# First retention layer: the compute engines' loop over sequences replaced by code written out for all sixteen

## The chip, the cores and the metric

The kernel runs on one core of a Trainium2 chip, as one program. The metric is the device time of one execution, in microseconds, lower is better. A core has five engines that run programs of their own and meet only at semaphores: TensorE (PE in the profile; its weight loads are PEld), VectorE (DVE), ScalarE (ACT), GpSimd (POOL) and SyncE (SP), which here only issues transfers. An engine's sequencer reads the engine's program, works out register values, waits on semaphores and hands instructions on.

## What is computed

Two layers, each a retention followed by a mixture of experts, on 16 sequences of 512 tokens with 128 features. The change touches the first retention alone:

```python
q, k = _apply_rotary((x @ Wq.T).reshape(B, T, 4, 32), (x @ Wk.T).reshape(B, T, 4, 32))
v = (x @ Wv.T).reshape(B, T, 4, 64)
q = q * 32 ** (-0.5)
scores = einsum('bhtd,bhsd->bhts', q, k) * decay_mask        # causal, one decay per head
o = einsum('bhts,bhsd->bhtd', scores, v)
o_n = o * rsqrt(mean(o * o, -1) + EPS) * g_norm_w
g = (x @ Wg.T).reshape(B, T, 4, 64)
x = layernorm(x + (o_n * silu(g)).reshape(B, T, 256) @ Wo.T)
# then: two of eight experts are chosen for each token of x
```

The kernel's first stage computes this, chooses the experts of every token and scatters the token rows to DRAM by expert. The experts of layer 0, the second retention, the experts of layer 1 and a last sum with its normalization follow as stages of their own.

## The kernel before

`retention0` gives each engine a program of steps. A step works on up to six sequences at once, each at another point of its way: `z` is sequence s (its transposed input is split in a high and a low part), `a` is s-1 (projections of q, k, v and the gate), `b` is s-2 (scores, states, outputs), `c` is s-3 (gating and transposes), `d` is s-4 (output projection, normalization, router), `e` is s-5 (ranks and rows of the chosen experts). POOL has a seventh, `f`, for s-6. So steps 0 to 20 carry the sixteen sequences through. Below, **score step n** is the stretch of TensorE's program from the scores of sequence n (L879, the first work of step n+2) to those of sequence n+1.

The engines are tied by semaphores that count up. What matters around the start of a score step: TensorE ends the step before with the transposes of `gated_transposes` (L917) and `outputs(b, 3)` (L898 and L901), then computes the scores (L879) into four banks, the ranks (L379 to L387) and the output projection (L937). ScalarE waits for L917 and copies the result (L734), then for `outputs(b, 3)` and squares it (L737). VectorE waits for that square, gates (L786) and masks the new scores (L762). TensorE needs the masked scores before it goes on to the projections of the next sequence (L863). Later in the step TensorE's transposes L330 need ScalarE's normalization L248.

`run_steps` (L79) writes a program. Steps below `2 * first` stand written out, each with the numbers of its sequences as constants. If `first < last`, one `Fori` (L92) follows whose body is two steps, run `last - first` times, with sequence numbers and semaphore counts taken from registers. The steps from `2 * last` on are written out again. In `retention0` `first, last = 3, SEQS // 2` (L603), that is 3 and 8: steps 0 to 5 written out, five iterations for steps 6 to 15, steps 16 to 20 written out. In score steps: 0 to 3 written out, 4 to 13 in the loop (two in an iteration, the even one first), 14 and 15 written out. POOL uses the same numbers; SyncE loops from step 10. `wait_count` (L60) and `Chain.link` (L77) make a wait with a count: of a constant, or in the loop of a register.

Of the kernel before, what the change touches and what calls it, by code (L numbers as in the profile page):

```python
# [16 lines left out]
SEQS, T, D = 16, 512, 128  # L17
# [31 lines left out]
def turn(i, sub, lag, count, unroll):  # L49

    k = sub - lag
    if isinstance(i, int):
        n = unroll * i + k
        return Turn(n, n // 2, n % 2, n // 4, n % 4) if 0 <= n < count else None
    if unroll == 4:
        return Turn(i * 4 + k, i * 2 + k // 2, k % 2, i + k // 4, k % 4)
    return Turn(i * 2 + k, i + k // 2, k % 2)

def wait_count(eng, sem, n):

    if isinstance(n, int) and n <= 0:
        return
    eng.wait_ge(sem, n)  # L63
# [19 lines left out]
def run_steps(eng, first, last, count, lags, body, between=(), unroll=2):  # L83


    total = count + max(lags)
    for s in range(unroll * first):
        body([turn(s // unroll, s % unroll, lag, count, unroll) for lag in lags])
        if s < len(between):
            between[s]()  # L90
    if first < last:
        with eng.Fori(first, last) as i:  # L92
            for sub in range(unroll):
                body([turn(i, sub, lag, count, unroll) for lag in lags])
    for s in range(unroll * last, total):
        body([turn(s // unroll, s % unroll, lag, count, unroll) for lag in lags])

def build(nc, x, x_T, w_proj, wo, gnorm, rope, router0, gate0, up0, down0,
# [9 lines left out]
    with whole:  # L108
# [422 lines left out]
        def retention0():  # L531
            ph = ExitStack()
            with ph:
# [68 lines left out]
                lags = [0, 1, 2, 3, 4]  # L602
                first, last = 3, SEQS // 2  # L603
# [5 lines left out]
                @block.sync  # L609
                def _(sp):  # L610
                    def load(t):

                        wait_count(sp, x_there, t.n - 1)
                        sp.dma_start(xT[t.odd][:], x_T[bass.ds(t.n, 1)].rearrange("b d t -> d (b t)")
                                     ).then_inc(s_x[t.odd], 16)

                    def body(ts):
                        if ts[0] is None:
                            return
                        load(ts[0])  # L620
                        if isinstance(ts[0].n, int) and ts[0].n == 0:
                            sp.dma_start(w_raw[:], w_proj).then_inc(s_wp, 16)
                            sp.dma_start(c_ident[:], ident).then_inc(s_id, 16)
                            for to, src in small:
                                sp.dma_start(to[:] if to is not w_r else to[:, 0:E], src).then_inc(s_w, 16)
                            for to, src in consts:
                                sp.dma_start(to[:], src).then_inc(s_const, 16)
                            sp.dma_start(tri_f[:], tri).then_inc(s_const, 16)
                        if isinstance(ts[0].n, int) and 1 <= ts[0].n <= 4:
                            q = ts[0].n - 1  # L630
                            sp.dma_start(xres[:, q * 16:(q + 1) * 16, :],
                                         x_seq[:, q * 4:(q + 1) * 4].rearrange("p b c d -> p (b c) d")
                                         ).then_inc(s_xr, 16)
                        if isinstance(ts[0].n, int) and 2 <= ts[0].n < 2 + E:
                            load_expert(sp, 0, ts[0].n - 2, s_wx0)

                    run_steps(sp, (2 + E) // 2, last, SEQS, [0], body)
                    tiles.fill(sp)
# [42 lines left out]
                @block.scalar  # L681
                def _(act):
                    def turned_logits(d):
                        act.wait_ge(lgT_mm, d.n + 1)
                        wait_count(act, router.lg_mm, d.n)
                        nc.scalar.copy(lgT[:], T1[:, 0:P]).then_inc(lgT_there, 1)

                    def body(ts):
                        z, a, b, c, d = ts
                        if b:  # L690
                            act.wait_ge(kt_mm, b.n + 1)
                            nc.scalar.copy(kt[:], T1[:, 0:(CH - 1) * P].rearrange("p (c k) -> p c k", c=CH - 1)
                                           ).then_inc(kt_ev, 1)
                        if z:
                            act.wait_ge(s_x[z.odd], z.half * 16 + 16)

                            wait_count(act, g_mm, z.n - 1)
                            nc.scalar.copy(x_hi[z.odd][:], xT[z.odd][:]).then_inc(x_hi_there, 1)
                        if c and not b:
                            act.wait_ge(ogT_mm, c.n + 1)  # L700
                            nc.scalar.copy(ogT[:], TT).then_inc(ogT_ev, 1)
                        if d:

                            wait_count(act, router.sent[d.odd], SCATTERS * d.half)
                            wait_count(act, x1_kept, d.n - 1)
                            norm.apply(act, r, x1[d.odd][:, :, 0:D], d, x1_there)
                        if a:
                            act.wait_ge(v_mm, a.n + 1)
                            nc.scalar.copy(v[a.odd][:], B01.rearrange("p b (c n) -> p (b c) n", c=2)).then_inc(v_ev, 1)
                        if b:  # L710

                            wait_count(act, ch_ss.sem, 2 * b.n - 1)
                            act.wait_ge(o_mm, 2 * b.n + 1)
                            nc.scalar.activation(osq[:, 0:2, :], O.rearrange("p (c n) -> p c n", c=2),
                                                 ACT.Square).then_inc(sq_there, 1)
                        if d:
                            act.wait_ge(router.tp, d.n + 1)
                            nc.scalar.copy(router.xT[:], T0).then_inc(router.xT_there, 1)
                            if not a:
                                turned_logits(d)  # L720
                            act.wait_ge(x1_there, d.n + 1)
                            nc.scalar.copy(xres[:, bass.ds(d.n * CH, CH), :], x1[d.odd][:, :, 0:D]).then_inc(x1_kept, 1)
                            router.copy_rows(act, d, x1_there)
                        if a:
                            act.wait_ge(g_mm, a.n + 1)

                            wait_count(act, og_there, 2 * (a.n - 1))
                            nc.scalar.activation(sg[a.odd][:], B23.rearrange("p b (c n) -> p (b c) n", c=2),
                                                 ACT.Silu).then_inc(g_ev, 1)
                        if d and a:  # L730
                            turned_logits(d)
                        if c and b:
                            act.wait_ge(ogT_mm, c.n + 1)
                            nc.scalar.copy(ogT[:], TT).then_inc(ogT_ev, 1)  # L734
                        if b:
                            act.wait_ge(o_mm, 2 * b.n + 2)
                            nc.scalar.activation(osq[:, 2:4, :], O.rearrange("p (c n) -> p c n", c=2),  # L737
                                                 ACT.Square).then_inc(sq_there, 1)

                    nc.scalar.preload_act_table_set("silu_and_others")  # L740
                    act.wait_ge(s_wp, 16)
                    nc.scalar.copy(w_hi[:], w_raw[:]).then_inc(w_hi_there, 1)
                    run_steps(act, first, last, SEQS, lags, body)

                @block.vector
                def _(dve):
# [97 lines left out]
                        if d:  # L844
                            router.choose(dve, LG, d)

                    run_steps(dve, first, last, SEQS, lags + [5], body)
                    tiles.table(dve)
                    centered.compute(dve)

# [1 line left out]
                def _(pe):  # L852
# [67 lines left out]

                    def body(ts):
                        _, a, b, c, d, e = ts
                        if b:

# [76 lines left out]
                        if b:  # L1001
                            outputs(b, 3)

                    run_steps(pe, first, last, SEQS, lags + [5], body)


        def experts(layer):
# [947 lines left out]
```

## Time and profile before

| | us |
|---|---|
| median of 3 runs | 1414.75 |
| lowest, highest | 1414.15, 1416.67 |
| the profiled execution | 1418.55 |
| its span in the trace | 1416.4 |

The profiled execution is 3.8 us longer than the median, and 2.15 us of it lie outside its span. The page gives busy times of engines over the span. A row of a window gives the same for a stretch; the timeline gives single instructions, with the idle time of the engine before one in brackets and what ended it: an instruction of another engine, "remote" for a semaphore whose raiser isn't told, or "issue" where the engine waited for nothing that the profile shows. In rows with a q behind the engine's name stands work of its sequencer, which isn't counted as busy.

### The profile page before, as it was taken

What the parts mean: (1) busy time and instruction counts of PE and PEld (TensorE: products, weight loads), DVE (VectorE), ACT (ScalarE), POOL (GpSimd) and SP (SyncE); (2) the same over time, 40 slices, a digit from 0 to 9 for tenths busy, and PEclk for the clock granted to TensorE, in tenths of its full rate; (3) what the DMA queues carried; (4) which work ended last, traced back from release to release, by engine and by line L of the source; (5) the groups of instructions that cost most, each with busy time, mean ns of one, the idle gap of its engine ahead of it and who ended that gap; (6) DMA issues with size and microseconds to landing.
All of it is one profiled execution on the core that took longest, in us unless ns stands there. A gap on an engine that the chain in (4) does not pass through costs nothing. (4 is left out here: it accounts for less than half of the span.)

```text
span 1416.4 us, 33456 instructions
## 1 busy us (share of the span) xinstructions
PE 1151.2 (81%) x10358; PEld 1023.1 (72%) x10359; DVE 911.9 (64%) x2572; ACT 718.5 (51%) x1875; POOL 746.8 (53%) x903
## 2 busy tenths in 40 slices
PE   7999999984188888846899999983499999999930
PEld 5887888864188788844676776662499999999930
DVE  4788788864465555514788888755566666666626
ACT  2344344432265555625566666642366666666627
POOL 0266667656446666651146666667244444444446
PEclk9999999986599998977999999985699999999975
DMA  7211112000232222214222112011221111111138
GB/s 230 58 60 45 43 45 71 26 24 31 84 90 88 80 83 82 84 40 141 76 91 84 58 58 75 28 35 58 57 57 53 54 54 56 52 54 54 42 112 266
DMA packets 75408, 102.00 MB, mean 72 GB/s; under 512 B 15154, under 2 KB 51506, under 8 KB 74866
## 3 DMA queue, kind: packets, MB, share of 16 engines
q1 hardware_dynamic: 49586, 60.96, 14.7%
q0 software_dynamic: 17280, 35.69, 7.7%
q10 hardware_dynamic: 8448, 4.20, 1.0%
q8 instruction: 48, 0.79, 0.2%
q14 instruction: 46, 0.38, 0.1%
HBM read 60.93 MB, written 44.11 MB: 74 GB/s over the span
## 5 line engine op out<-in xcount | busy, mean ns | idle before, releaser
L1091 POOL DMA_INDIRECT expert_out<-e_ysb,e_idx x284 | 309.2, 1089 | 309.1 <-ACT e_ysb L1130 180.5
L1239 PE MATMUL banks<-e_x_hi,e_w_hi 128*128 128x256 f32 x852 | 255.9, 300 | 4.6 <-issue 2.4
L1239 PE MATMUL banks<-e_x_hi,e_w_lo 128*128 128x256 f32 x852 | 244.0, 286 | 2.2 <-issue 2.0
L1239 PE MATMUL banks<-e_x_lo,e_w_hi 128*128 128x256 f32 x852 | 243.7, 286 | 2.5 <-issue 2.5
L1249 PE MATMUL banks<-w_dn,e_h 128*128 x1704 | 220.5, 280 | 19.2 <-issue 9.9
L1210 DVE TENSOR_TENSOR e_h<-banks,e_sgl 128x512 f32<-128x512 f32 x213 | 146.8, 690 | 137.0 <-PE banks L1239 75.7
L1249 PEld LDWEIGHTS banks<-w_dn,e_h 128*128 128x128 f32 x1704 | 207.4, 195 | 22.3 <-issue 22.1
L1117 ACT ACTIVATE e_sgl<-banks 128x512 f32<-128x512 f32 x213 | 128.1, 602 | 122.9 <-PE banks L1239 80.0
L1239 PEld LDWEIGHTS banks<-e_x_hi,e_w_hi 128*128 128x128 f32 x852 | 165.9, 195 | 5.8 <-issue 5.7
L1239 PEld LDWEIGHTS banks<-e_x_hi,e_w_lo 128*128 128x128 f32 x852 | 165.5, 194 | 4.7 <-issue 4.7
L1239 PEld LDWEIGHTS banks<-e_x_lo,e_w_hi 128*128 128x128 f32 x852 | 166.0, 195 | 2.8 <-issue 2.6
L1200 DVE TENSOR_TENSOR e_w_lo<-w_gu,e_w_hi 128x512 fp32r<-128x512 f32 (+1 forms) x142 | 136.4, 960 | 39.8 <-ACT e_w_hi L1108 28.9
L451 POOL DMA_INDIRECT scattered<-b_r_x,b_r_idx x128 | 131.1, 1025 | 36.5 <-issue 36.2
L451 POOL DMA_INDIRECT scattered<-a_r_x,a_r_idx x128 | 128.7, 1005 | 36.3 <-issue 36.3
L1108 ACT CAST e_w_hi<-w_gu 128x512 fp32r (+1 forms) x142 | 119.8, 844 | 8.0 <-issue 6.0
L1226 PE MATMUL banks<-c_ident,e_xg 128*128 128x128 f32 x284 | 57.1, 284 | 59.0 <-DMA e_xg<-scattered 58.6
L1111 ACT CAST e_x_hi<-banks 128x256 fp32r<-128x256 f32 x142 | 53.4, 376 | 97.3 <-PE banks L1226 52.2
L1531 DVE TENSOR_TENSOR b_sT<-banks,c_causal 128x1024 f32<-128x1024 f32 x64 | 75.4, 1220 | 23.2 <-PE banks L1609 22.0
L1226 PEld LDWEIGHTS banks<-c_ident,e_xg 128*128 128x128 f32 x284 | 36.7, 147 | 62.1 <-issue 52.3
L1204 DVE TENSOR_TENSOR e_x_lo<-banks,e_x_hi 128x256 fp32r<-128x256 f32 x142 | 59.6, 420 | 29.7 <-ACT e_x_hi L1111 23.1
L664 POOL TENSOR_TENSOR a_inv_rms<-a_mse,c_half 128x16 f32<-128x16 f32 x16 | 53.5, 3341 | 47.6 <-DVE a_mse L779 46.5
L901 PEld LDWEIGHTS banks<-a_v,a_sT 128*128 128x128 f32 x512 | 69.6, 197 | 4.3
(280 smaller groups left out, 2468.7 us busy)
## 6 DMA issues: line engine op xcount, KB each, us to landing
e_xg<-scattered SPq DMA_DIRECT2D x142, 130.0 KB, 1.9
b_cy<-expert_out SPq DMA_DIRECT2D x32, 256.0 KB
f_y<-expert_out SPq DMA_DIRECT2D x32, 256.0 KB, 3.9
expert_out<-e_ysb,e_idx POOLq DMA_INDIRECT x284
a_xT<-in_x_T SPq DMA_DIRECT2D x16, 256.0 KB
out<-f_x ACTq DMA_DIRECT2D x16, 256.0 KB, 4.1
scattered<-in_spare SPq DMA_DIRECT2D x2, 1040.0 KB
scattered<-in_spare SPq DMA_DIRECT2D x16, 130.0 KB
```

What stands on the lines that cost most here:

```text
L451: nc.gpsimd.indirect_dma_start(out=scattered[0:E * REGION, :], out_offset=bass.IndirectOffsetOnAxis(ap=self.idx[t.odd][:, j:j + 1], axis=0 ...
L901: mm = nc.tensor.matmul(O[:, at + h * DV0:at + (h + 1) * DV0], sT[:, h, c, :], v[b.odd][:, c, h * DV0:(h + 1) * DV0], start=(c == 0 and h ...
L1091: nc.gpsimd.indirect_dma_start(out=expert_out, out_offset=bass.IndirectOffsetOnAxis(ap=idx[d.slot][:, i:i + 1], axis=0), in_=ysb[d.slot][: ...
L1108: nc.scalar.copy(w_hi[b.slot][:], w_gu[:, bass.ds(e, 1), :, 0:F].rearrange("p o g f -> p (o g) f")).then_inc(w_hi_there, 1)
L1117: nc.scalar.activation(sgl[bank_of(j, c)][:], GB[bank_of(j, c)][:].rearrange("p (k n) -> p k n", k=2), ACT.Silu).then_inc(sg_there, 1)
L1200: nc.vector.tensor_tensor(w_lo[b.slot][:], w_gu[:, bass.ds(e, 1), :, 0:F].rearrange("p o g f -> p (o g) f"), w_hi[b.slot][:].bitcast(F32), ...
L1204: nc.vector.tensor_tensor(x_lo[b.slot][:], TP[b.odd][:, 0:ROWS], x_hi[b.slot][:].bitcast(F32), ALU.subtract).then_inc(x_ev, 1)
L1210: nc.vector.tensor_tensor(h[c.slot][:, 2 * j:2 * j + 2, :], UB[bank_of(j, c)][:].rearrange("p (k n) -> p k n", k=2), sgl[bank_of(j, c)][:] ...
L1226: mm = nc.tensor.transpose(TP[b.odd][:, i * P:(i + 1) * P], xg[b.slot][:, i, 0:D], c_ident[:])
L1239: mm = nc.tensor.matmul(banks[bank_of(j, c)][:, i * ROWS:(i + 1) * ROWS], w_[c.slot][:, g, f:f + P], x_[c.slot][:], start=(k == 0), stop=( ...
L1249: mm = nc.tensor.matmul(YB[d.odd][:, i * D:(i + 1) * D], h[d.slot][:, f, i * P:(i + 1) * P], w_dn[:, bass.ds(e, 1), f, :].rearrange("p o d ...
L1531: nc.vector.tensor_tensor(sT[h][:, 2 * g:2 * g + 2, :, :].rearrange("p g n t -> p (g n) t"), pairs[2 + g].rearrange("p g (n t) -> p (g n) ...
```

## The change

The programs of ScalarE, VectorE and TensorE in `retention0` are made with `run_steps(..., last, last, ...)` in place of `run_steps(..., first, last, ...)`, so the branch with `Fori` isn't taken and all 21 steps stand written out. GpSimd's and SyncE's programs, the order of the work within a step, buffers, and the other stages stay as they are.

```diff
@@ retention0, scalar
-                    run_steps(act, first, last, SEQS, lags, body)
+                    run_steps(act, last, last, SEQS, lags, body)
@@ retention0, vector
-                    run_steps(dve, first, last, SEQS, lags + [5], body)
+                    run_steps(dve, last, last, SEQS, lags + [5], body)
@@ retention0, tensor
-                    run_steps(pe, first, last, SEQS, lags + [5], body)
+                    run_steps(pe, last, last, SEQS, lags + [5], body)
```

What stands on TensorE after the ranks in the loop's second step, before the change (the names in brackets are semaphores; L946 and L950 set up a wait for the masked scores, L954 one for the outputs' bank):

```order
L943 MATMUL banks<-c_ident,a_kT 128x128 [waits a_ogT_ev]
L943 MATMUL banks<-c_ident,a_kT 128x128 x2
L946 ISA
L950 REGISTER_ALU [waits a_sT_there]
L863 MATMUL banks<-a_x_hi,a_w_hi 128x512 [waits a_x_there]
```

and in a step of the changed kernel:

```order
L943 MATMUL banks<-c_ident,a_kT 128x128 [waits a_ogT_ev]
L943 MATMUL banks<-c_ident,a_kT 128x128 x2
L863 MATMUL banks<-a_x_hi,a_w_hi 128x512 [waits a_x_there,a_sT_there]
```

The two register instructions are gone and the wait on the masked scores stands on the matrix multiply itself.

On ScalarE, at the entry of the loop and in the first step of its body, before the change:

```order
L737 ACTIVATE a_osq<-banks 128x512 [waits a_o_mm]
L92 UNCONDITIONAL_BRANCH
L92 ISA
L692 COPY a_kt<-banks 128x384 [waits a_kt_mm]
L695 ISA
L698 CAST a_x_hi<-a_xT 128x512 [waits a_g_mm,a_x0]
L63 ISA
L63 REGISTER_ALU [waits sent00]
L246 REGISTER_ALU [waits a_x1_kept]
L248 ACTIVATE a_r_x<-a_r,a_n_bias,a_n_rstd 128x128 [waits a_n_inv]
```

and at the same place of the changed kernel:

```order
L737 ACTIVATE a_osq<-banks 128x512 [waits a_o_mm]
L692 COPY a_kt<-banks 128x384 [waits a_kt_mm]
L698 CAST a_x_hi<-a_xT 128x512 [waits a_g_mm,a_x0]
L248 ACTIVATE a_r_x<-a_r,a_n_bias,a_n_rstd 128x128 [waits a_n_inv,a_x1_kept,sent00]
```

The branch and the register instructions are gone; copies, activations and their waits stand in the order in which they stood.

## Rows read from the trace of the kernel before

**Rows 1.** The page's head and part 1: busy time, share, instructions of each engine.

```profile
span 1416.4 us, 33456 instructions
PE 1151.2 (81%) x10358; PEld 1023.1 (72%) x10359; DVE 911.9 (64%) x2572; ACT 718.5 (51%) x1875; POOL 746.8 (53%) x903
```

**Rows 2.** Windows, one for each of score steps 3 to 14: start:end, length, busy times.

```profile
68.26:85.97 17.71, 17.57 (x179) 15.30 (x179) 15.93 (x54) 8.13 (x15) 8.36 (x9) 1.00 0.15 46
...
85.97:105.13 19.16, 18.09 (x180) 15.62 (x179) 15.40 (x51) 7.37 (x15) 13.56 (x17) 1.00 0.21 65
105.13:124.97 19.84, 18.50 (x179) 15.74 (x179) 15.97 (x53) 8.14 (x15) 13.54 (x17) 1.00 0.20 61
124.97:144.91 19.94, 18.52 (x179) 15.75 (x178) 16.01 (x54) 8.15 (x15) 13.55 (x17) 1.00 0.13 40
144.91:163.98 19.07, 17.93 (x180) 15.48 (x179) 15.90 (x53) 8.14 (x15) 13.55 (x17) 1.00 0.13 42
163.98:183.94 19.96, 18.56 (x180) 15.77 (x179) 16.32 (x56) 8.14 (x15) 13.55 (x17) 1.00 0.12 40
183.94:203.09 19.15, 18.17 (x179) 15.72 (x178) 15.66 (x51) 8.14 (x15) 13.54 (x17) 1.00 0.14 42
203.09:223.02 19.93, 18.51 (x179) 15.75 (x178) 16.40 (x54) 8.13 (x15) 13.63 (x17) 1.00 0.13 40
223.02:242.10 19.08, 17.93 (x179) 15.49 (x178) 16.00 (x54) 8.14 (x15) 13.55 (x17) 1.00 0.27 82
242.10:261.44 19.34, 18.05 (x180) 15.61 (x179) 16.43 (x56) 8.27 (x16) 13.55 (x17) 1.00 0.13 43
261.44:280.48 19.04, 17.94 (x179) 15.57 (x179) 15.93 (x54) 8.10 (x15) 13.55 (x17) 1.00 0.09 28
280.48:299.60 19.12, 18.14 (x179) 15.69 (x178) 15.69 (x54) 8.50 (x15) 13.43 (x16) 1.00 0.10 33
```

The columns behind the length are PE, PEld, DVE, ACT and POOL busy time with instructions, then TensorE's granted clock, the DMA share and GB/s.

**Rows 3.** The loop's own line L92, whole program: sequencer instructions, duration ns min/median/max.

```profile
L92 PEldq COMPARE_BRANCH  x23: 83/215/238, 122.8 to 1319.3; - x23
L92 DVEq COMPARE_BRANCH  x25: 50/56/85, 125.6 to 1406.4; - x25
L92 ACTq COMPARE_BRANCH  x25: 40/45/59, 126.5 to 1406.9; - x25
```

**Rows 4.** Timelines of ACT and of DVE as score steps 7 and 8 begin.

```profile
145.45 1.01 ACT L734 COPY a_ogT<-banks 128x1024 f32<-128x1024 f32 x1 [3.32 <-remote]
165.33 1.01 ACT L734 COPY a_ogT<-banks 128x1024 f32<-128x1024 f32 x1 [4.06 <-remote]
...
147.00 0.69 DVE L786 TENSOR_TENSOR a_og<-banks,a_sg 128x512 f32<-128x512 f32 x1 [1.40 <-ACT a_osq L737]
166.96 0.69 DVE L786 TENSOR_TENSOR a_og<-banks,a_sg 128x512 f32<-128x512 f32 x1 [2.21 <-ACT a_osq L737]
```

**Rows 5.** Waits of PE over the loop, 85.97:280.48: us in total, times, longest.

```profile
PE banks L330 <- ACT a_r_x L248: 7.8, 10, 0.9
PE banks L879 <- issue: 3.5, 10, 0.4
```

**Rows 6.** DMA queues of the first pass through the loop's body, 85.97:124.97: packets, MB, share.

```profile
q8 instruction: 3, 0.05, 0.5%
q14 instruction: 2, 0.02, 0.2%
```

**Rows 7.** DMA queues of the later passes, 120:285.

```profile
q1 hardware_dynamic: 1616, 3.29, 6.8%
q14 instruction: 1, 0.01, 0.0%
```

**Rows 8.** The queue q8 in the windows 104.5:105 and 299.8:300.3.

```profile
q8 instruction: 1, 0.02, 11.7%
...
q8 instruction: 1, 0.02, 12.0%
```

**Rows 9.** PE's timeline: end of the scores in score steps 14 and 15.

```profile
282.66 0.58 PE L937 MATMUL banks<-a_won,a_ogT 128*128 128x128 f32 x3
...
302.30 0.40 PE L879 MATMUL banks<-a_qr,a_kT 32*128 32x128 f32 x3 [0.94 <-issue]
306.66 1.63 PE L937 MATMUL banks<-a_won,a_ogT 128*128 128x128 f32 x6
```

## The prediction

> **What bounds the kernel now.** I read the page first: TensorE is busy 81% of the span, the next engine 64% [rows 1]. Then the windows of the stage that is changed, cut at the starts of the scores [rows 2]. In each score step TensorE is busy 17.9 to 18.6 of 19.04 to 19.96 us, VectorE 15.4 to 16.4, GpSimd 13.6, ScalarE 8, and the granted clock is 1.00 (2.4 GHz), so the step goes by TensorE with what it waits for. The reader is to see a pattern in the lengths. Steps 4 to 13 are the loop. The first steps of iterations two to four, which are 6, 8 and 10, take 19.94, 19.96 and 19.93 us; the second steps 7, 9, 11 and 13 take 19.07, 19.15, 19.08 and 19.04. Two don't fit: step 5, a second one, takes 19.84, and step 12, a first one, only 19.34. Step 4, entered without a jump back, takes 19.16. Step 14, written out on all three engines, takes 19.12.
>
> Where the 0.8 us of a long step lie is in the timelines of its start. In step 7 (from 144.91) ScalarE's L734 begins 0.54 us after the scores, in step 8 (from 163.98) 1.35 us after. VectorE's L786 follows at +2.09 and +2.98, idle 1.40 and 2.21 us before it [rows 4]. That delay reaches the masked scores and TensorE's next projections. ScalarE had long been idle, so it is a result of TensorE that comes late by that much. The waits that the profile names on TensorE are the same kind in every step: L330 for ScalarE, 7.8 us in ten steps, and 3.5 us of "issue" inside the scores [rows 5].
>
> **Part 1, the jump back.** On TensorE one L92 branch lasts 215 ns at the median and 238 at most, on VectorE 56, on ScalarE 45 [rows 3]. The work of the latter two hides that: both wait for TensorE around the step's start, 1.40 us even in a short step [rows 4]. On TensorE's own side the branch comes just ahead of the scores, 32 small products that need instructions fast. Four jumps back at 0.24 us are 0.95 us, the lower bound of the gain if the step lengths have another cause. The upper bound is from the step lengths. The loop lasts from 85.97 to 280.48, 194.51 us for ten steps; ten steps like step 14 would be 191.20. The difference is **3.31 us**: 0.76 in iteration one (39.00 less 38.24), 0.77, 0.87, 0.77, and 0.14 in the last. I take the upper value, since the jump back precedes just steps 6, 8, 10 and 12, three of which are 0.8 us longer than their neighbours with the same instructions, and since step 14, even as they are, is short. What is late next in a step of 19.1 us is the chain through VectorE's statistics, GpSimd's power and L248 to L330, which is there in step 14 too.
>
> **Part 2, register instructions.** Waits that were built from registers become waits on constants: on TensorE two or so of the sequencer's instructions go at five places of a step, on the others likewise. A second step of an iteration has these too, and at 19.04 to 19.15 us it is as long as step 14, which has none. So I cost their removal at nothing. What hides it is the time that a long product takes while the sequencer reads on. If that cover is absent at the scores, it is in the 3.5 us of issue time over ten steps [rows 5], and these are the most that it could bring.
>
> **Part 3, code.** The loop's body is fetched once: three packets of queue q8, TensorE's, and two of q14 in the 39.00 us of its first pass [rows 6]. In 120:285, over four more passes, q8 has no packet at all and q14 one [rows 7]. Written out, the eight further steps fetch about four times as much: 12 packets on q8 and 8 or so on q14. As transfers these are nothing, each a few hundredths of a MB. But does TensorE halt when it goes on to a new piece? The steps 0 to 3 and 14 have such fetches and no gap that I can tie to them. Against that, two fetches fall right at the start of scores: one in 104.5:105, ahead of step 5 (105.13), the odd step that is long; and one in 299.8:300.3, in step 15 [rows 8], where TensorE gets its instructions so slowly that L937 begins 7.06 us after the scores' start and not 2.18 as in step 14 [rows 9]. Price of one hit: nothing at the low end, 0.77 us (step 5 less step 7), 4.88 at the high end (7.06 less 2.18). I take nothing, for step 15 has another cause at hand (GpSimd's scatters, unpaced there). The Trainium skill, page "Runtime: NRT & Kernel Launch", section "Instruction fetch mechanics", holds that a sequencer fetches the next block while it runs the present one and that crossing is mostly hidden, which would speak for nothing too. The same section says that a taken branch breaks the prefetch if its target isn't among the pages held and that kernels for this reason rather unroll. By that each of the four jumps back would have its own fetch, and the trace disagrees for TensorE: q8 has none in 120:285 [rows 7].
>
> **Part 4, what isn't changed.** GpSimd and SyncE keep their loops. GpSimd is paced by the others' semaphores and busy 13.6 us of a step [rows 2], so it follows a shorter one. The stage ends in a chain that starts from the last scores, and the following stages start when all engines are through, so 3.3 us saved ahead of step 14 reach the end.
>
> **Sum.** Against the profiled execution: 1418.55 - 3.31 = 1415.24. The same saving from the median of the runs, 1414.75, gives 1411.44; I forecast **1411.5 us**. A measurement here tells about 0.2%, 2.8 us, from no change; the forecast is barely beyond it.
>
> **The rivals.**
>
> *Fetches eat part of the gain.* Of 12 new fetches, if they fall evenly and those within 2 us of the start of the scores count (4 of 19.1 us), 2.5 hit, at 0.77 us 1.9 us; step 5's own 0.77 stays. 3.31 - 0.77 - 1.9 = 0.6 us: **1414.1**. For it: step 5, which no jump explains. Against it: steps 0 to 3.
>
> *The pattern isn't the jump's.* Even and odd sequences use different buffers, and the even ones could be slower by something else in the middle of the stage, or the delay appears only with the profiler on. For it: step 12 follows a jump too and is 0.27 us longer, not 0.8. Against it: step 14 is even and short. Then nothing changes: **1414.7**.
>
> *The change makes it slower.* TensorE's code is no longer all held once the loop has gone round, and a piece that begins in the middle of the scores while GpSimd scatters costs what step 15 lost, 4.88 us [rows 9]. Two such hits in ten steps are 9.8, less 3.3: 1414.75 + 6.5 = **1421**. It decides from one such hit on, since 4.88 is more than 3.31. For it: the fetch lies within 0.7 us of the stall's begin. Against it: step 5, hit likewise, lost 0.77 at most, and GpSimd's unpaced scatters are in step 15 alone.
>
> *More is gained.* Step 3, written out, with the same 179 products, takes 17.71 us [rows 2]. If the loop made all of the difference to 19.1, ten steps would give 14 us more: **1397**. Against it: step 14 is written out and takes 19.12; step 3 differs in GpSimd's load (8.36 us, not 13.6).
>
> **How the numbers follow.** Chances: the forecast 0.43, fetches eating part 0.25, no effect 0.15, slower 0.11, more gained 0.06. The forecast's own range is 1409.5 to 1412.5: below, the issue time of part 2 half saved; above, a third of the gain lost. The range of 8 in 10 also takes in the second and the third case with a run's spread of 1 to 2 us above them, since the runs went from 1414.15 to 1416.67: 1409.2 to 1416.2. Faster by over 0.2% (below 1411.9): 0.37 of the forecast's 0.43, and more gained, 0.43. Within: 0.06, 0.24 and 0.14, so 0.44. Slower: 0.11 and 0.02 of the others, 0.13.
>
> **What would show it.** Right: score steps 5 to 13 all at 19.0 to 19.2 us, L734 about 0.6 us behind the scores' start in even and odd steps alike, some 20 fetches of q8 in the stage, and step 15 as long as before. Rival one: long steps remain, and a fetch of q8 stands within 2 us of each one's start. Rival two: 19.9 us at even steps still. Slower: gaps of issue inside L879 of over 0.9 us, several in a row, in steps before 15. Wrong in another way would be a change after the stage's end, near 388 us: later stages run the same code, but the fetches of TensorE fall at other places in them.

## The result, and the profile after

| | before | changed |
|---|---|---|
| median of 20 runs each, us | 1419.97 | 1414.51 |
| lowest, highest | 1414.15, 1426.18 | 1409.76, 1419.31 |
| profiled execution, us | 1418.55 | 1415.69 |
| its span | 1416.4 | 1413.9 |

The ratio of the changed kernel to the kernel before is 0.9951, 95% interval 0.9935 to 0.9967: faster by 0.49%, or by 4.7 to 9.2 us from end to end of the interval. The medians differ by 5.5. The median of before has moved as well: over 20 runs it is 1419.97, where the first three gave 1414.75.

The page of the changed kernel has the same compute work as [rows 1] and more pieces of code:

```profile
span 1413.9 us, 33103 instructions
PE 1150.6 (81%) x10358; PEld 1022.6 (72%) x10359; DVE 910.2 (64%) x2572; ACT 716.5 (51%) x1875; POOL 742.6 (53%) x903
...
q8 instruction: 59, 0.97, 0.3%
q14 instruction: 51, 0.42, 0.1%
```

Some 350 instructions are gone, none of them on an engine's data path: the counts behind the busy times are those of [rows 1]. The score steps, which answer to [rows 2] (windows by score step 3 to 14; columns as there):

```profile
66.29:84.01 17.72, 17.57 (x180) 15.31 (x179) 15.94 (x54) 8.28 (x15) 8.36 (x9) 1.00 0.16 46
84.01:103.03 19.02, 18.06 (x179) 15.59 (x179) 15.61 (x52) 7.22 (x14) 13.53 (x17) 1.00 0.21 65
103.03:122.15 19.12, 17.98 (x179) 15.53 (x179) 16.32 (x56) 8.14 (x15) 13.53 (x17) 1.00 0.21 63
122.15:141.30 19.15, 18.01 (x180) 15.57 (x179) 15.94 (x54) 8.29 (x16) 13.55 (x17) 1.00 0.14 43
141.30:160.32 19.02, 17.99 (x180) 15.54 (x179) 15.60 (x52) 8.17 (x16) 13.55 (x17) 1.00 0.14 44
160.32:179.38 19.06, 17.97 (x180) 15.59 (x179) 16.29 (x56) 8.28 (x16) 13.51 (x17) 1.00 0.13 43
...
274.52:293.52 19.00, 18.00 (x179) 15.63 (x178) 15.42 (x53) 7.67 (x15) 13.41 (x16) 1.00 0.10 33
```

No step is long now: score steps 4 to 13 take from 84.01 to 274.52, 190.51 us where they took 194.51, and step 14 takes 19.00 where it took 19.12. Step 3, the same code in both kernels, is 17.71 and 17.72.

The starts of steps 7 and 8, on ScalarE and VectorE, which answer to [rows 4]:

```profile
141.14 1.01 ACT L734 COPY a_ogT<-banks 128x1024 f32<-128x1024 f32 x1 [2.56 <-PE banks L917]
142.71 0.60 ACT L737 ACTIVATE a_osq<-banks 128x512 f32<-128x512 f32 x1 [0.55 <-PE banks L901]
...
160.22 1.01 ACT L734 COPY a_ogT<-banks 128x1024 f32<-128x1024 f32 x1 [2.63 <-PE banks L917]
161.77 0.60 ACT L737 ACTIVATE a_osq<-banks 128x512 f32<-128x512 f32 x1 [0.54 <-PE banks L901]
...
143.33 0.69 DVE L786 TENSOR_TENSOR a_og<-banks,a_sg 128x512 f32<-128x512 f32 x1 [1.92 <-ACT a_osq L737]
162.40 0.69 DVE L786 TENSOR_TENSOR a_og<-banks,a_sg 128x512 f32<-128x512 f32 x1 [1.54 <-ACT a_osq L737]
```

L734 begins 0.16 and 0.10 us ahead of the scores (141.30, 160.32), where it began 0.54 and 1.35 behind. L786 is at +2.03 and +2.08, where it was at +2.09 and +2.98. So at L786 a short step has gained 0.06 us and a long one 0.9.

The 2.5 us between the two spans don't all belong to the change. Up to score step 4 the changed kernel's trace is 1.96 us shorter, where both kernels run the same code; score steps 4 to 14 are 4.12 us shorter; and from score step 15 on, 1116.8 us became 1120.4, 3.6 us longer.

### The profile page after: what moved, and what is told of

It reads as the page before. It is cut to its first block and busy times, and to the rows that moved or that the text cites. A ratio compares the mean times of both kernels' runs of the same rounds, so it can differ in the third digit from the quotient of the medians.

```text
span 1413.9 us, 33103 instructions
## 1 busy us (share of the span) xinstructions
PE 1150.6 (81%) x10358; PEld 1022.6 (72%) x10359; DVE 910.2 (64%) x2572; ACT 716.5 (51%) x1875; POOL 742.6 (53%) x903
## 5 line engine op out<-in xcount | busy, mean ns | idle before, releaser
L1204 DVE TENSOR_TENSOR e_x_lo<-banks,e_x_hi 128x256 fp32r<-128x256 f32 x142 | 59.5, 419 | 23.5 <-ACT e_x_hi L1111 17.4
L901 PEld LDWEIGHTS banks<-a_v,a_sT 128*128 128x128 f32 x512 | 69.4, 197 | 4.0
```

Of the source, the lines that this page charges most:

```text
L901: mm = nc.tensor.matmul(O[:, at + h * DV0:at + (h + 1) * DV0], sT[:, h, c, :], v[b.odd][:, c, h * DV0:(h + 1) * DV0], start=(c == 0 and h ...
L1204: nc.vector.tensor_tensor(x_lo[b.slot][:], TP[b.odd][:, 0:ROWS], x_hi[b.slot][:].bitcast(F32), ALU.subtract).then_inc(x_ev, 1)
```

## The experiments

They ran in three groups; the kernels of a group shared a chip and the runs of the kernel before. The median of before was 1420.23 us in the first group, 1411.99 in the second and 1412.65 in the third, so times are compared within a group. The same holds for traces: a short step takes about 19.05 us in the first group and 18.9 in the other two. The second group has no trace of before or of the changed kernel. What tells most is the trace: the sum of score steps 4 to 13, taken from the start of one L879 group to another's.

### Which engine

**TensorE alone written out.**

```diff
-                    run_steps(pe, first, last, SEQS, lags + [5], body)
+                    run_steps(pe, last, last, SEQS, lags + [5], body)
```

> TensorE alone is written out in the first retention; VectorE and ScalarE keep their loop. Theory (the 0.8 us of a long score step is TensorE's jump back, just ahead of the scores): score steps 4 to 13 sum to about 190.5 to 191.2 us as in the changed kernel (190.5) and not 194.5 as before, and the whole is faster than before by what the full change brings. Rival (VectorE's and ScalarE's jumps and register waits make the delay): the sum stays near 194.5, and the time at that of before.

Measured: sum 191.44 us, no long step; ratio 0.9967 (0.9946 to 0.9988). The sum is 0.2 us above what the theory gave.

**VectorE and ScalarE alone written out.**

```diff
-                    run_steps(act, first, last, SEQS, lags, body)
+                    run_steps(act, last, last, SEQS, lags, body)
...
-                    run_steps(dve, first, last, SEQS, lags + [5], body)
+                    run_steps(dve, last, last, SEQS, lags + [5], body)
```

> VectorE and ScalarE are written out in the first retention, TensorE keeps its loop. Theory (TensorE's jump): score steps 4 to 13 sum to 194 to 195 us, with 19.9 us in steps 6, 8 and 10, and the time is that of before. Rival (the other two engines): the sum is near 190.5 us and all of the gain is here.

Measured: sum 191.69 us; ratio 0.9960 (0.9936 to 0.9983). Step 6 alone is long.

**The changed kernel and the kernel before, once more.**

> The changed kernel once more, for its spread. If the first retention alone makes the difference, its score steps 4 to 13 again sum to 190.5 us within 0.5, the start of the kernel up to score step 4 and the stages behind the first retention differ from trace to trace by one to three us for both kernels, with no direction. If the later stages changed too, the expert stage of layer 0 is again some 2 us longer than before.

> The kernel before once more, for its spread. Theory: score steps 4 to 13 sum to 194.5 us within 0.5, again with long steps 6, 8 and 10; the time is within 0.1% of before. Rival (the pattern of long and short steps was that one execution's): other steps are long, and the sum lies anywhere between 190.5 and 196.

Measured: sums 190.47 and 194.13 us. In the second trace of before steps 6, 8 and 10 take 19.99, 20.03 and 19.98 us, step 5 takes 19.16 and not 19.84. Ratios 0.9956 (0.9932 to 0.9980) and, for the kernel before against itself, 0.9988 (0.9965 to 1.0011). The expert stage of layer 0, 2.2 us longer in the changed kernel's first trace (246.7 and 248.9 from its first product to its last scatter), isn't longer in its second (248.0, and 248.4 in before's), so no change behind the first retention is shown.

The loop as one window each, of the kernel before again, the changed kernel again, TensorE alone, and VectorE with ScalarE (columns as in [rows 2]):

```profile
84.33:278.46 194.13, 182.32 (x1781) 156.89 (x1780) 160.03 (x530) 80.64 (x150) 135.57 (x161) 1.00 0.15 48
...
84.50:274.97 190.47, 180.02 (x1781) 155.71 (x1780) 159.56 (x531) 81.42 (x150) 135.63 (x161) 1.00 0.16 50
...
83.50:274.94 191.44, 180.00 (x1781) 155.53 (x1780) 160.03 (x530) 80.65 (x150) 135.26 (x161) 1.00 0.16 50
...
85.64:277.33 191.69, 180.96 (x1781) 156.24 (x1780) 159.66 (x531) 80.92 (x151) 135.23 (x161) 1.00 0.16 49
```

Either half of the change brings most of it: 2.9 and 2.6 us of 3.8, reckoned from the mean 194.32 of the two traces of before. The parts don't add. Against the changed kernel's trace of the same group (190.47) the loops of VectorE and ScalarE cost 1.0 us while TensorE is written out, TensorE's loop 1.2 while the other two are, and all three together 3.7. That fits neither theory as written: the jump of TensorE isn't always enough for a long step (in the second kernel one of four steps behind it is long), and the loops of the other two alone give none (the first has them).

ScalarE's timeline shows why. L734 waits for `ogT_mm`, which TensorE raises after L917. Step 6 of the kernel with VectorE and ScalarE written out (scores from 123.69), and of that with TensorE written out (from 121.71):

```profile
125.05 1.01 ACT L734 COPY a_ogT<-banks 128x1024 f32<-128x1024 f32 x1 [4.07 <-remote]
125.96 0.60 ACT L737 ACTIVATE a_osq<-banks 128x512 f32<-128x512 f32 x1
...
122.34 1.01 ACT L734 COPY a_ogT<-banks 128x1024 f32<-128x1024 f32 x1 [3.35 <-remote]
123.25 0.60 ACT L737 ACTIVATE a_osq<-banks 128x512 f32<-128x512 f32 x1
```

It starts at +1.36 in one and at +0.63 in the other. Taken over score steps 5 to 14 of all traces but that with the scatters moved (below), L734 begins near -0.15, near 0.6 or near 1.35 us behind the scores' start and never between: three levels, 0.73 us apart (some 0.1 us earlier in the second and third group, where a fourth, near -0.95, comes up seven times). ScalarE isn't what is slow: by the trace's semaphore events `ogT_mm` is raised 0.02 to 0.03 us before L734 begins, at every level, while the last product of L917 ends 1.20 us ahead of the scores in every step (such ends are modelled). The second result, which L737 waits for, is there at 1.2 to 1.5 us whatever the level. So with L734 at -0.15 or 0.6, its 1.01 us are over by 1.6 and L737 starts at 1.25 to 1.55. At 1.35 they are over at 2.3, and L737, L786 and the masked scores are 0.8 us late. TensorE's projections (L863), which need the masked scores, then begin at 4.86 us and not 4.14 (steps 8 and 7 of before), and L248 at 11.54 and not 10.73.

This account covers all long steps but one. In these 130 steps L734 is at the third level 12 times, and these take 19.78 to 20.03 us; the other 118 take 18.85 to 19.36, with one exception of 19.81. TensorE's jump ahead of the scores goes with it: 11 of the 12 follow one (8 of 12 such steps in three traces of the kernel before, 3 of 8 with ScalarE, or VectorE and ScalarE, written out, none of 4 with jumps put into the changed kernel), and the twelfth is step 5 of the first trace. What the loops of VectorE and ScalarE add is seen in the kernel with TensorE alone written out: L734 is at 0.56 to 0.63 in steps 5 to 12, where the changed kernel has it near -0.15 in most, and its steps take 19.05 to 19.23 us. By what way a jump or a loop of another engine delays TensorE's result isn't shown.

### Is it the jump or the registers

**Five loops of one pass.** Register waits and code length stay, the jump back goes.

```diff
+    for at in range(first, last):
+        with eng.Fori(at, at + 1) as i:
+            for sub in range(unroll):
+                body([turn(i, sub, lag, count, unroll) for lag in lags])
```

> The kernel before, but on TensorE, VectorE and ScalarE five loops of one pass each stand in place of one loop of five: each pass keeps its register instructions and has an entry, none jumps back to its start, and the code is as long as that of the changed kernel. Theory (the jump back is what costs): score steps 4 to 13 sum to 190.5 to 191.5 us, the changed kernel's length. Rival (register instructions and waits on registers cost, or a loop's entry costs as a jump does): the sum is 194 us, with 19.9 us in even steps.

Measured: sum 189.55 us, no long step; ratio 0.9965 (0.9944 to 0.9985). The branch instruction itself stays, but isn't taken, and lasts 67 ns on TensorE. That the sum is below the changed kernel's 190.5 isn't a gain: that was another group. L734 is at 0.48 to 0.55 in the even steps, which stand behind a loop's entry, and at -0.93 to -0.21 in the odd ones. So an entry goes with a level too, only not the third.

**TensorE's loop turned by half a step.** All three engines loop. `run_halves` calls the second half of step s and the first half of step s+1, twice in an iteration.

```diff
+    front(at(unroll * first))
+    with eng.Fori(first, last) as i:
+        for sub in range(unroll):
+            back([turn(i, sub, lag, count, unroll) for lag in lags])
+            front([turn(i, sub + 1, lag, count, unroll) for lag in lags])
+    back(at(unroll * last))
...
                             project_all(B[3], a, 3).then_inc(k_mm, 1)
+
+                    def back(ts):
```

> The kernel before with all three loops, but TensorE's is turned by half a step: its jump back stands behind the projections of k (L863), in the middle of long products, and no longer ahead of the scores. Theory (TensorE's jump costs because the short products behind it want instructions fast): score steps 4 to 13 sum to 191.4 us, as with TensorE written out alone, and L734 begins 0.6 us behind the scores' start, not 1.35, in every even step. Rival (VectorE's and ScalarE's loops bring the delay, or a jump costs wherever it is): steps 6, 8 and 10 take 19.9 us, sum 194.

Measured: sum 190.81 us; steps 6, 8 and 10 are short, step 12 takes 19.81; ratio 0.9996 (0.9960 to 1.0032). Step 12 isn't a long step of the kind above: L734 begins at 0.53 and L737 at 1.43. Here it is a later result that is told late, that of the projections of q: the last of these products ends 5.82 us behind the scores' start (5.69 in step 10), and VectorE's L809, which waits for it, begins at 7.24 and not at 6.46; L248 follows at 11.39 and not at 10.59 (line numbers of the kernel before). TensorE's jump stands at 5.33 us now, and GpSimd has transfers from 4.93 to 5.90 and from 6.21 to 7.18. That looks like the same lateness at another place, but one step doesn't show it.

**ScalarE alone written out.**

```diff
-                    run_steps(act, first, last, SEQS, lags, body)
+                    run_steps(act, last, last, SEQS, lags, body)
```

> ScalarE alone written out. VectorE and ScalarE together brought the sum of score steps 4 to 13 to 191.7 us. Theory A: it is ScalarE, whose copy L734 is the instruction that is late: the sum is 191.7. Theory B: it is VectorE: the sum is 194.3 as before. Theory C: whether L917's result is told at 0.6 or 1.35 us is a near thing, which any of the three engines tips by a few hundredths: single even steps lose their 0.8 us and others keep it, the sum lies between, at 192 to 193.5.

Measured: sum 191.57 us, with steps 8 and 10 at 19.85 and 19.78 and step 6 at 19.04; ratio 1.0031 (1.0003 to 1.0059). The sum is theory A's, the pattern is C's. How much of the loop's gain this is can't be said, with no trace of before in its group; one of the next group has 191.99. The kernel's time is longer than before's. Its second retention takes 388 us in the one trace (below), so its whole time can't be put to the edit. No run has VectorE alone written out.

**The same with before beside it.** The third group has a trace of the kernel before, and the turned loop again.

> The kernel before once more, to stand beside the three that follow on one chip. Theory (L917's result is told at one of three moments, some 0.73 us apart, and TensorE's jump pushes it to the last): score steps that follow a jump, 6, 8, 10, are 19.8 to 20.0 us with L734 at 1.2 to 1.4 us, the others 18.9 to 19.2; sum of 4 to 13 194 us. On a chip where it is a nearer thing one or two of the three may be short: 192 to 194.

> TensorE's loop turned by half a step once more, beside a trace of the kernel before on the same chip. Theory: all three engines loop, yet the sum of score steps 4 to 13 is 190.5 to 191.5 us with at most one long step, and lies 2 to 4 us under the kernel before's. Rival: the short sum of the last trace was that chip's, and both are alike here.

Measured: sums 191.99 and 190.17 us; ratios 1.0010 (0.9985 to 1.0035) and 0.9998 (0.9969 to 1.0026). The turned loop lies 1.8 us under the kernel before, a little less than the 2 to 4 expected. On this chip the kernel before has two long steps, 6 and 10, so the loop has less to lose here than the 3.8 us of the first group. Its steps 6 to 9:

```profile
123.33:143.19 19.86, 18.53 (x179) 15.75 (x178) 16.01 (x54) 8.34 (x16) 13.51 (x17) 1.00 0.12 40
143.19:162.12 18.93, 17.93 (x179) 15.50 (x178) 15.99 (x54) 8.03 (x15) 13.52 (x17) 1.00 0.13 42
162.12:181.28 19.16, 18.07 (x180) 15.66 (x179) 16.32 (x56) 8.34 (x16) 13.52 (x17) 1.00 0.14 42
181.28:200.23 18.95, 17.93 (x179) 15.49 (x178) 15.68 (x52) 8.02 (x15) 13.52 (x17) 1.00 0.14 42
```

and ScalarE as its steps 6 (from 123.33) and 8 (from 162.12) begin:

```profile
124.58 1.01 ACT L734 COPY a_ogT<-banks 128x1024 f32<-128x1024 f32 x1 [3.98 <-remote]
125.49 0.60 ACT L737 ACTIVATE a_osq<-banks 128x512 f32<-128x512 f32 x1
...
162.67 1.01 ACT L734 COPY a_ogT<-banks 128x1024 f32<-128x1024 f32 x1 [3.27 <-remote]
163.58 0.60 ACT L737 ACTIVATE a_osq<-banks 128x512 f32<-128x512 f32 x1
```

The same program and the same jump give +1.25 in one step and +0.55 in the next but one, and with them 19.86 and 19.16 us. Thus a jump doesn't have a price of 0.8 us; it raises the odds of one. With TensorE's jump ahead of the scores, eight of twelve steps are long by a late L917, over three traces of before (steps 6, 8, 10 and 12 each); with it in mid-step, none of eight is over two traces, while VectorE and ScalarE still loop.

**Jumps put into the changed kernel.**

```diff
                         if b:
                             outputs(b, 3)
+                            if b.n in (5, 7, 9, 11):
+                                with pe.Fori(0, 2):
+                                    pass
```

> The changed kernel, with an empty loop of two passes, one jump back in each, put in TensorE's program ahead of the scores of score steps 6, 8, 10 and 12, where the kernel before has its jumps. VectorE and ScalarE stay written out. Theory (TensorE's jump delays the telling of L917): L734 of these four steps begins 0.5 to 0.6 us behind the scores' start and no longer at -0.15, in one or more of them at 1.3, which makes that step 0.8 us longer; sum 190.9 to 193.8, against 190.5 without. Rival (a jump on TensorE alone costs nothing, and it was the length of the loop's code or its register waits): L734 at -0.15 and a sum of 190.5.

Measured: sum 189.56 us, no long step; ratio 0.9962 (0.9938 to 0.9986). The last kernel of this group, whose first retention is the changed kernel's, has 189.27. Step 6 (from 122.25) begins so:

```profile
122.75 1.01 ACT L734 COPY a_ogT<-banks 128x1024 f32<-128x1024 f32 x1 [3.21 <-remote]
123.66 0.60 ACT L737 ACTIVATE a_osq<-banks 128x512 f32<-128x512 f32 x1
```

L734 is at 0.50, 0.54, -0.20 and 0.56 us in steps 6, 8, 10 and 12. Without the jumps, in the last kernel of this group, it is at -0.22, -0.24, -0.95 and 0.49. In three of four steps it is one level higher with the jump, and the second level costs little: 19.07 us where the first has 18.92, in the mean of this group. But this is one trace of each, and in steps without a jump the two traces differ by a level as well, once up and three times down in steps 5, 7, 9, 11 and 13. Nor does the edit part a jump from a loop's entry, which goes with the second level in the loops of one pass. In these four steps a jump on TensorE, with the other engines written out, doesn't reach the third level. The expectation that one or more steps would be long has missed.

**The second retention written out too**, on top of the changed kernel, for a faster version.

```diff
-                    run_steps(pe, first, last, SEQS, lags, body)
+                    run_steps(pe, last, last, SEQS, lags, body)
```

and likewise for `act` and `dve` in `retention1`.

> The changed kernel with the second retention's programs of TensorE, VectorE and ScalarE written out too (three jumps back fewer on each). Theory (a jump costs only where short products and a late result follow it, and the second retention's length varies by several us from one execution to the next for another reason): the time is that of the changed kernel within 0.2%, or 1 to 3 us less. Rival (what was gained in the first retention is gained again in proportion): 3 us less. If code fetches cost there: 1 to 3 us more.

Measured: median 1406.71 us, ratio 0.9957 (0.9929 to 0.9985). The kernel with jumps put in has 1406.89 and 0.9962 in the same group, so nothing beyond the first retention's gain is shown. Against before of this group the loop of the first retention is 2.7 us shorter (191.99 and 189.27).

### What makes TensorE's results late

**GpSimd's second pair of scatters moved** from the end of a sequence's step to the begin of the next, on top of the changed kernel.

```diff
-                                router.scatter_pair(pool, f, 2, sc_mm, b.n + 1)
+                                router.scatter_pair(pool, f, 1, sc_mm, b.n + 1)
...
+                            router.scatter_pair(pool, f, 2)
                             router.scatter_pair(pool, f, 3)
...
-                            if z:
-                                router.scatter_pair(pool, e, 1, router.tp, d.n + 1)
-                            else:
+                            if not z:
```

> The changed kernel, with GpSimd's second pair of scatters of a sequence moved from the end of its step to the begin of the next, behind the scores. Theory (TensorE's results come late at a step's start because GpSimd starts indirect transfers during the short products ahead of it): L737 begins about 0.1 us behind the scores' start, as in score steps 1 to 3, and not 1.4 us; the step's length may still not fall, since GpSimd's power for L248 now stands behind three pairs and ends some 0.3 to 1 us later: 18.5 to 19.3 us a step. Rival (GpSimd has no part in it): L737 still begins at 1.4 us.

Measured: ratio 1.0070 (1.0043 to 1.0097), sum 204.05 us. ScalarE's timeline at score step 7 (from 145.85; line numbers are one less in this file), and PE's and ACT's waits over the loop (us in total, times, longest):

```profile
144.69 1.01 ACT L733 COPY a_ogT<-banks 128x1024 f32<-128x1024 f32 x1 [1.63 <-PE banks L916]
145.96 0.60 ACT L736 ACTIVATE a_osq<-banks 128x512 f32<-128x512 f32 x1 [0.26 <-PE banks L900]
...
PE banks L887 <- DVE a_S L768: 25.9, 20, 1.5
...
ACT a_r_x L248 <- DMA scattered<-a_r_x,a_r_idx: 18.2, 3, 6.4
```

The copy of L917 starts at -1.16 us and the square of L901 at +0.11, in every one of steps 4 to 14. Nothing is late any more and there are no levels. In the changed kernel GpSimd has a transfer in each of the stretches -3.05 to -1.92, -1.55 to -0.57 and -0.26 to +0.7 us around a score step's start; here the last two are gone, and the first alone does no harm. So it is GpSimd's indirect transfers, running while TensorE goes through its short products, that make TensorE's results come late and in levels 0.73 us apart. Score steps 2 and 3 of every kernel, which have no such transfer at their start, agree: -1.16 and +0.11.

But the step isn't shorter. It takes 20.1 us, where 18.5 to 19.3 were expected: the state products wait for VectorE, 1.3 us twice a step. Steps 8 and 12 take 21.6; in these the granted clock is 0.92 and TensorE busy for 19.1 and 18.9 us, in the others 1.00 and 17.4 to 17.6. L248's waits for a scatter, up to 6.4 us, are no more than 0.7 above the 5.75 that ScalarE is idle there in the other steps. The theory of the lateness holds; what an end to it would be worth isn't shown, nor that it makes the difference between step 3 (17.7 us) and the others.

## Why the prediction was right, and where it was not

**The direction and the size.** The forecast was 3.3 us less; the loop lost 3.8 us in the mean of two traces of each kernel (194.32 and 190.50), step 14 another 0.13, and the runs 5.5 (4.7 to 9.2 by the interval). The forecast value of 1411.5 was 3 us low, from two errors that offset each other: the base of 1414.75 was 5.2 us too low, since the kernel before has a median of 1419.97 over 20 runs, and the saving was 2.2 too small. From the right base the same saving gives 1416.7, above the range's end of 1416.2. That the range held 1414.51 is in part luck.

**Part 1, the jump back: right sum, half the mechanism.** "Ten steps like step 14" was a good estimate, 191.20 where 190.5 came. But 0.76 of its 3.31 us is iteration one, whose long step 5 no jump precedes; in the second trace of before that step is short, 19.16. The pattern behind the jumps was real: 6, 8 and 10 are long in that trace too, and 11 of 12 steps with the late L917 follow a jump of TensorE ahead of the scores.

Two steps of the argument failed. "The work of the latter two hides that" reckoned the loops of VectorE and ScalarE at nothing since both wait for TensorE. With TensorE written out they still cost 1.0 us (191.44 and 190.47), and with these two written out and TensorE's loop kept, two of three long steps went. The other is the reason given, that the scores behind the branch need instructions fast. The branch stands 2.12 us ahead of the scores, and it isn't the supply of instructions that is late: the last product of L917 ends 1.20 us ahead of the scores in short and long steps alike, and what comes late is the raising of its semaphore, while GpSimd's transfers run. With these moved away it is on time in each step. The lower bound of 0.24 us a jump had no meaning either: a jump ahead of the scores costs 0.8 us when it goes with the third level, in 11 of 24 cases, and little when it doesn't.

**Part 2, register instructions: mis-sized.** I costed them at nothing because second steps of an iteration were as long as step 14. Yet step 14, whose own code didn't change, fell from 19.12 and 19.15 to 19.00 in both traces, and step 13 stayed at 19.04. Of the 0.7 us by which the loop beat my 191.20, all is steps at 19.0 to 19.1 instead of 19.12. But the register instructions needn't be the cause: L734 in step 14 went from 0.60 and 0.63 to -0.17, and in the third group, where before has it at -0.19 already, step 14 takes 18.94 us in before and 18.91 in the last kernel. So this gain goes with the level as well. The sign I gave, L734 about 0.6 us behind the scores in all steps, missed: in steps 7 to 14 of the changed kernel it is 0.10 to 0.17 ahead. The issue time inside the scores fell from 3.5 us [rows 5] to

```profile
PE banks L879 <- issue: 2.9, 10, 0.4
```

which is 0.6 us and fits, without being shown to be the cause.

**Part 3, code: right.** In the loop's stretch of the changed kernel q8 has 14 packets, one less than reckoned (three, and 12 more):

```profile
q8 instruction: 14, 0.23, 0.6%
...
q8 instruction: 1, 0.02, 7.4%
...
q8 instruction: 1, 0.02, 8.3%
```

The second and third row are of the windows 141.8:142.8 and 275.9:276.6, each about 1 to 2 us behind the start of a score step (141.30 and 274.52). These steps take 19.02 and 19.00 us. So a fetch in the midst of the short products costs nothing here, and the rival that had fetches eat the gain is out, with that of the slower kernel. Step 5's 19.84 us, its only witness, came from one execution: in the next trace of before the fetch stands 0.60 us ahead of that step, where it was 0.45, and the step takes 19.16. The Trainium skill, page "Runtime: NRT & Kernel Launch", section "Instruction fetch mechanics", has crossings from one such piece to the next as mostly hidden; these rows agree, at 19.02 and 19.00 us. Step 15's stall stayed: L937 begins at 300.72, 7.20 us after the scores' start at 293.52, and 7.06 before [rows 9].

**Rival two** (the pattern isn't the jump's) is out by the changed kernel, by the one whose TensorE jumps in mid-step and by the loops of one pass. **More gained**: steps like step 3 need GpSimd's scatters out of the way, as I had held against it, and even then other waits take their place.

**Part 4, later stages: open.** The profiled execution gained 2.86 us and not 4, and the runs more than 4. Between the first retention's loop and the end lie stages whose lengths differ from trace to trace. Up to score step 4 a trace takes 83.5 to 84.5 us with a granted clock of 1.00, or 85.3 to 86.0 with one of 0.98, in kernels of both sorts (a single one has 85.6 at 1.00); here before and changed:

```profile
0.00:85.97 85.97, 73.91 (x658) 63.11 (x660) 57.38 (x137) 30.80 (x49) 17.30 (x27) 0.98 0.44 128
...
0.00:84.01 84.01, 71.61 (x659) 61.44 (x660) 57.38 (x137) 30.95 (x49) 17.29 (x27) 1.00 0.44 131
```

The stage of the second retention, from the last scatter of the first expert stage to the first work of the second, in the kernel before, in that with ScalarE written out, in that with TensorE written out and in the changed one:

```profile
631.56:1007.39 375.83, 291.23 (x2966) 218.12 (x2967) 259.21 (x919) 196.44 (x615) 194.57 (x329) 0.89 0.22 69
...
625.00:1013.32 388.32, 308.00 (x2967) 230.29 (x2967) 258.34 (x919) 195.93 (x615) 194.70 (x329) 0.84 0.21 67
...
627.35:1001.83 374.48, 291.73 (x2966) 218.16 (x2967) 258.71 (x919) 195.99 (x615) 194.24 (x329) 0.88 0.22 69
...
628.58:1005.51 376.93, 293.68 (x2967) 219.99 (x2967) 258.41 (x919) 196.15 (x615) 194.18 (x328) 0.88 0.22 69
```

The same code takes 374.5 to 388.3 us, and the longest goes with the lowest clock. That is more than the change is worth; the intervals of the ratios are 4.5 to 10 us wide. Where the 1.5 us between the traces' 4.0 and the runs' 5.5 come from isn't settled. The turned loop has 1.8 us less in the loop than before on its chip and a ratio of 0.9998, with an interval that neither shows that gain nor excludes it. One trace a kernel can't tell whether the place of TensorE's code has a part in the second retention's length.

## What to carry to other kernels

Compare the lengths of equal steps before costing anything: here the step written out among looped ones gave the loop's gain to within a fifth in the first group of traces, while the price of the branch instruction gave a quarter of it. Ask next what ends late and by how much it may be late for free. A delay that lands ahead of a free moment costs nothing, the same delay a level later costs all of it, and then small edits on different engines each seem to bring most of the gain.

A step that is long in one trace, once, is not a witness. A second trace of the kernel before would have taken from the fetch rival the ground for its chance of 0.25. And take the base from more than three runs: here it was 5 us off, as much as the change is worth.

## What the runs showed of the hardware

- While GpSimd starts indirect transfers (about 1 us each), TensorE's results in a run of short products are told (their semaphore is raised) up to 2.5 us late on a first waiting instruction and 1.2 to 1.4 us on a second. On the first the delay comes in levels 0.73 us apart: L734 starts at -1.16 us without the transfers, and near -0.15, 0.6 or 1.35 with them. L737 starts at +0.11 without and at 1.25 to 1.55 with them, where L734 doesn't hold it up.
- Of 24 steps with a jump back of TensorE ahead of the scores, 11 had L734 at the highest level; of the 106 others in the same thirteen traces, one had. A jump back that is taken lasts 215 ns on TensorE at the median (before), one that isn't 67 ns (loops of one pass).
- A fetch of 16 KB of TensorE's code, 14 times in the 190.5 us of code written out, cost no time that shows, even at the begin of the scores (19.02 and 19.00 us). A body of two steps, three such pieces long, was not fetched again on later passes in before; one packet came late in a trace of the turned loop, at 166.69.
